# Decoder layer on one core: one-transfer query maxima, a ninth weight slot, weight loads spread over the last batch, and the router's mask in PSUM

## The reference

```python
x = x + mixer(layernorm(x))            # cumulative sums over tokens, low-rank products
x = x + xattn(layernorm(x), ctx_512)   # 16 heads of 32, softmax(Q K^T / sqrt(32)) V, Wo
x = x + ffn(layernorm(x))              # 32 experts

# ffn, per batch:
probs = softmax(x @ gate_w.T + gate_b, axis=tokens)
vals, idx = top 8 tokens of each expert
merged = sum over the 8 of vals * x[idx]              # one vector per batch and expert
h = gelu([merged, 1] @ w1)     # w1: (32, 513, 2048)
o = [h, 1] @ w2                # w2: (32, 2049, 512)
out[idx] += vals * o
```

## Time and profile before

| | us |
|---|---|
| median of 3 runs (2260.3 to 2263.67) | 2262.58 |
| the profiled execution | 2257.76 |
| its span, first to last instruction | 2256.1 |
| PE / DVE / ACT / POOL busy in the span | 1858.3 / 1028.3 / 745.9 / 823.6 |
| DMA moved | 421.34 MB, mean 187 GB/s |

### The profile page before, as it was taken

One profiled execution on the slowest core, in us unless ns is written; L12 is line 12 of the kernel. 1 busy time (PEld: TensorE's weight loads), 2 busy tenths in 40 slices (PEclk: granted clock), 3 DMA queues, 4 the chain that ended last, 5 costly groups with the idle time before them and its releaser, 6 DMA issues. The chain is left out here.

```text
span 2256.1 us, 41492 instructions
## 1 busy us (share of the span) xinstructions
PE 1858.3 (82%) x12594; PEld 1211.7 (54%) x12594; DVE 1028.3 (46%) x2541; ACT 745.9 (33%) x1551; POOL 823.6 (37%) x591
## 2 busy tenths in 40 slices
PE   7889999999999999999999999976756656556544
PEld 5667777677677776777777777753211111111111
DVE  1355766667667666666676666642100000000003
ACT  3144444445445444454454543532100000000000
POOL 0255555545555555465555555543000000000000
PEclk9799999999999999999999999977878787787776
DMA  5324333333243243332432433364899999999996
GB/s 172 88 67 109 78 77 95 82 87 95 74 106 77 76 97 81 89 96 74 103 78 76 99 80 82 80 223 146 367 418 421 421 420 423 422 420 421 422 377 252
DMA packets 143265, 421.34 MB, mean 187 GB/s; under 512 B 33036, under 2 KB 79084, under 8 KB 118652
## 3 DMA queue, kind: packets, MB, share of 16 engines
q1 hardware_dynamic: 135580, 411.70, 53.4%
q10 hardware_dynamic: 6656, 8.15, 1.0%
q0 software_dynamic: 992, 1.02, 0.1%
HBM read 307.37 MB, written 17.14 MB: 144 GB/s over the span
## 5 line engine op out<-in xcount | busy, mean ns | idle before, releaser
L1139 DVE TENSOR_REDUCE maxes<-bank 112x1 f32<-112x376 f32 (+1 forms) x1024 | 511.1, 537 | 129.6 <-PE bank L1345 127.0
L943 ACT ACTIVATE probs<-bank 125x448 f32<-125x448 f32 x768 | 399.5, 546 | 156.9 <-PE bank L1367 150.0
L1367 PE MATMUL bank<-q_st,k_st 98*125 98x224 f32 x1536 | 338.6, 307 | 23.5 <-DMA q_st<-max_lo 21.9
L821 POOL TENSOR_TENSOR psum_keys<-psum_keys,probs 125x896 f32<-125x896 f32 x127 | 266.6, 2099 | 214.9 <-ACT probs L943 209.8
L1345 PE MATMUL bank<-k_st,q_st 96*112 96x376 f32 (+1 forms) x1024 | 319.6, 358 | 21.5 <-DVE maxes L1139 18.9
L1753 PE MATMUL bank<-ring,hid_T 128*32 128x512 f32 x1024 | 175.5, 848 | 194.2 <-DMA ring<-in_L_ffn_w 191.0
L1367 PEld LDWEIGHTS bank<-q_st,k_st 98*125 98x125 f32 x1536 | 258.3, 192 | 82.2 <-issue 48.1
L1671 DVE TENSOR_TENSOR o_fin<-bank,b_row 16x512 f32<-16x512 f32 x32 | 21.7, 679 | 586.0 <-PE bank L1711 586.0
L824 POOL TENSOR_TENSOR psum_keys<-psum_keys,probs 125x896 f32<-125x896 f32 x127 | 266.7, 2100 | 9.9
L1593 POOL DMA_DIRECT2D o_rows<-o_fin x31 | 15.2, 492 | 597.7 <-DVE o_fin L1671 597.7
L1345 PEld LDWEIGHTS bank<-k_st,q_st 96*112 96x112 f32 x1024 | 170.2, 181 | 77.9 <-DVE maxes L1139 50.3
(11 more groups left out here) (168 smaller groups left out, 2762.4 us busy)
## 6 DMA issues: line engine op xcount, KB each, us to landing
ring<-in_L_ffn_w SPq DMA_DIRECT2D x128, 2048.0 KB, 30.4
k_st<-k_hi SPq DMA_DIRECT2D x512, 93.8 KB, 2.1
k_st<-k_lo SPq DMA_DIRECT2D x256, 93.8 KB, 2.2
q_st<-q_hi SPq DMA_DIRECT2D x504, 28.0 KB, 1.8
ctx_nat<-in_ctx SPq DMA_DIRECT2D x16, 750.0 KB
x_in<-in_x SPq DMA_DIRECT2D x16, 448.0 KB, 3.7
out<-x SPq DMA_DIRECT2D x16, 448.0 KB, 3.1
out<-ring ACTq DMA_DIRECT2D x28, 256.0 KB, 3.0
```

Of the source, the lines that this page charges most:

```text
L821: nc.gpsimd.tensor_tensor(psum_keys[:], psum_keys[:], lo, ALU.add).then_inc(pool_chain, 1)
L943: nc.scalar.activation(probs[n % 2][:, j, :], bank[5 + u % 2][0:SK, 0:2 * T], ACT.Exp, scale=SCALE).then_inc(probs_ready, 1)
L1139: nc.vector.tensor_reduce(maxes[:, j, t, c:c + 1], score_bank(n)[0:TT, 0:SC[c + 1] - SC[c]], AX.X, ALU.max).then_inc(s_drained, 1)
L1367: last = nc.tensor.matmul(bank[5 + u % 2][0:SK, kk * T:(kk + 1) * T], k_st[slot][:, j, k * SK:(k + 1) * SK], q_st[slot][:, j, :], start=Tr ...
```

## The change

Four things:

1. *Maxima in one transfer.* `join_maxima` writes each maximum twice ([112, 16]), `turn_max` gives 16 partitions, and `max_rows` makes one tile `max_two` whose first 8 partitions are the high part and whose last 8 are the low part (a column `low_half` of zeros and ones tells them apart). `stack_max` moves both rows with one transfer.
2. *Mask in PSUM.* `beaten` is now the second half of the PSUM bank in which the job `gate` left the logits.
3. *Ninth slot.* `wv_lo`, `ctx_lo`, `xh` and `bias_row` move into a ninth slot of the ring (`EXTRA`). In the last batch SP also loads expert 2's first chunk there, so that 9 chunks are in before the experts start; the turn for experts 2 and 3 is written out, reads that chunk from the extra slot and doesn't refill slot 0. After that the ninth slot is not used.
4. *Order of loads and of the experts' start.* The last batch's loads go out as 0, 1, 2 in group 0, 3, 4 in group 1, 5 and the extra one in group 2, 6 in group 3, each behind the first unit of its group, and 7 after the last unit. `tok` is cleared in the first phase; DVE takes both tokens first; PE turns the biases after the first expert's first matrix.

```diff
+                def extra_weight():
+                    sp.wait_ge(yt_ready, 2 * B)
+                    sp.wait_ge(x_bias_ready, B)
+                    sp.wait_ge(chunk_in[0], 16)
+                    load_chunk(sp, 2, 0, None, 0)
+                def last_batch_weights(kt):
+                    if kt == 0:
+                        sp.wait_ge(x1_ready, 2 * B)
+                        first_weights([0])
...
+                        first_weights([1, 2])
+                    elif kt == 1:
...
+                        first_weights([3, 4])
+                    elif kt == 2:
+                        first_weights([5])
+                        extra_weight()
+                    else:
+                        first_weights([6])
...
+                        if kind == "last":
+                            sp.wait_ge(scores_ready, (LAST * 4 + kt) * 12 + 1)
+                            last_batch_weights(kt)
...
-                        if kind == "last" and kt >= 2:
-                            sp.wait_ge(scores_ready, (LAST * 4 + kt - 1) * 12)
-                            first_weights([2 + kt])
...
-                    for r, part in enumerate((max_hi, max_lo)):
-                        row = 3 * HD + r
-                        act.dma_start(q_st[slot][row:row + 1, :, :].rearrange(
-                            "o j (t n) -> o (j t) n", t=2).bitcast(F32), part[:, :].bitcast(F32)
-                                     ).then_inc(max_stacked[slot], 16)
+                    act.dma_start(q_st[slot][3 * HD:3 * HD + 2, :, :].bitcast(F32),
+                                  max_two[:].bitcast(F32)
+                                  ).then_inc(max_stacked[slot], 16)
...
+                def beaten(kind):
+                    return bank_of("gate", kind)[0:E, T:2 * T]
...
-                    nc.vector.scalar_tensor_tensor(out=weight[0:E, :], in0=beaten[:], scalar=NEG,
+                    nc.vector.scalar_tensor_tensor(out=weight[0:E, :], in0=beaten(kind), scalar=NEG,
...
-                    nc.vector.tensor_reduce(q_max[:], maxes[:].rearrange("p j t c -> p (j t) c"),
+                    twice = maxes[:].rearrange("p j t c -> p (j t) c").unsqueeze(1)
+                    nc.vector.tensor_reduce(q_max[:].rearrange("p (r q) -> p r q", r=2),
+                                            twice.to_broadcast([TT, 2, 8, 2]),
                                             AX.X, ALU.max).then_inc(q_max_ready, 1)
...
-                    nc.vector.tensor_scalar(max_hi[:], bank[4][0:8, 0:TT], -1.0, None, ALU.mult
-                                            ).then_inc(max_hi_ready, 1)
-                    dve.wait_ge(max_hi_ready, g + 1)
-                    nc.vector.scalar_tensor_tensor(out=max_lo[:], in0=bank[4][0:8, 0:TT],
-                                                   scalar=-1.0, in1=max_hi[:].bitcast(F32),
-                                                   op0=ALU.mult, op1=ALU.subtract
-                                                   ).then_inc(max_ready, 1)
+                    nc.vector.tensor_copy(max_hi[:], bank[4][0:16, 0:TT]).then_inc(max_hi_ready, 1)
+                    dve.wait_ge(max_hi_ready, g + 2)
+                    nc.vector.scalar_tensor_tensor(out=max_two[:], in0=max_hi[:].bitcast(F32),
+                                                   scalar=low_half[:, 0:1],
+                                                   in1=bank[4][0:16, 0:TT], op0=ALU.mult,
+                                                   op1=ALU.subtract).then_inc(max_ready, 1)
...
-                with sp.Fori(1, E // 2 - 1) as i:
+                weights(1, 0, False, (1, 2, 3))
+                weights(1, 1, False)
+                with sp.Fori(2, E // 2 - 1) as i:
...
                 take(0, 0, True)
+                take(0, 1, True)
...
+                expert(1, 0, False, EXTRA)
+                expert(1, 1, False)
```

More of the change, by code:

```diff
@@ L109, in build @@
     assert N_MID % 2 == 0
+    assert all(q.index("wt0") - q.index("gate") <= 2 for q in (SEQ["mid"], SEQ["last"], SEQ["tail"]))
     def place(job, kind):
@@ L155, in build, with home_of @@
         SLOTS = 8
+        EXTRA = 4
+        def home_of(slot):
+            return slot if slot < EXTRA else slot + 1
         D1, H1 = KD * P, H
@@ L437, in _, with load_chunk @@
                                                 ).then_inc(s_lo, 1)
-        def load_chunk(sp, e, q, slot):
+        def load_chunk(sp, e, q, slot, told=None):
             n = 2 * H
+            done = chunk_in[slot if told is None else told]
+            slot = home_of(slot) if told is None else EXTRA
             if q < 2:
@@ L444, in load_chunk @@
                 sp.dma_start(ring[:, slot, :], src[:, q * n:(q + 1) * n]
-                             ).then_inc(chunk_in[slot], 16)
+                             ).then_inc(done, 16)
                 return
@@ L492, in build @@
         z_mix = sb(lay, "z_mix", [P, T])
-        beaten = z_mix[0:E, :]
         weight = sb(lay, "weight", [P, T])
@@ L1632, in _ @@
             def _(dve):
-                for c in range(HC):
-                    part = slice(c * 32, (c + 1) * 32)
-                    nc.vector.tensor_copy(adder[part, :], ident[part, part]
-                                          ).then_inc(adder_ready, 1)
-                dve.wait_ge(b1_flipped, 1)
-                nc.vector.tensor_copy(b1_T[:].rearrange("p t c e -> p (t c e)"), bank[4][:]
-                                      ).then_inc(b1_ready, 1)
                 dve.wait_ge(cleared, 1)
@@ L1674, in _ @@
                 take(0, 0, True)
+                take(0, 1, True)
+                for c in range(HC):
+                    part = slice(c * 32, (c + 1) * 32)
+                    nc.vector.tensor_copy(adder[part, :], ident[part, part]
+                                          ).then_inc(adder_ready, 1)
+                dve.wait_ge(b1_flipped, 1)
+                nc.vector.tensor_copy(b1_T[:].rearrange("p t c e -> p (t c e)"), bank[4][:]
+                                      ).then_inc(b1_ready, 1)
                 add_biases(0, 0, True)
-                take(0, 1, True)
                 row_out(0, 0, True)
@@ L1696, in _, with flip_biases @@
             def _(pe):
-                pe.wait_ge(b1_loaded, 16 * HC)
-                for t in range(HT):
-                    last = nc.tensor.transpose(bank[4][:, t * P:(t + 1) * P],
-                                               b1_rows[:].rearrange("e (p t) -> e t p", t=HT)[:, t, :],
-                                               ident[:])
-                last.then_inc(b1_flipped, 1)
-                pe.wait_ge(adder_ready, HC)
+                def flip_biases():
+                    pe.wait_ge(b1_loaded, 16 * HC)
+                    for t in range(HT):
+                        last = nc.tensor.transpose(
+                            bank[4][:, t * P:(t + 1) * P],
+                            b1_rows[:].rearrange("e (p t) -> e t p", t=HT)[:, t, :], ident[:])
+                    last.then_inc(b1_flipped, 1)
                 def sum_parts(i, e2, first):
@@ L1708, in sum_parts @@
                     pe.wait_ge(o_copied, e + 1)
-                    if not first:
+                    if first:
+                        pe.wait_ge(adder_ready, HC)
+                    else:
                         pe.wait_ge(o_out, e)
@@ L1712, in sum_parts, with expert @@
                                      start=True, stop=True).then_inc(o_summed, 1)
-                def expert(i, e2, first):
+                def expert(i, e2, first, extra=None):
                     e = i * 2 + e2
@@ L1723, in expert @@
                             pe.wait_ge(chunk_in[slot], i * 16 + 16)
+                        slot = home_of(slot)
+                        if extra is not None and kd < 2:
+                            slot = extra
                         for c in range(HC):
@@ L1730, in expert @@
                     last.then_inc(h_full, 1)
+                    if first and e2 == 0:
+                        flip_biases()
                     if e2 == 1:
```

71 lines of the change are left out of this document (34 added, 37 removed).

## The result

The changed kernel takes 2225.88 us (median of 4 runs, 2225.29 to 2228.49) against 2262.26 us (2260.3 to 2263.67) for the kernel before: ratio 0.9842, 95% interval 0.9825 to 0.9859. It is 36.4 us faster where 24.7 were forecast, and 2225.9 lies just under the range's lower end of 2227. A second measurement later gave 2228.48 against 2259.05 us, ratio 0.9875 (0.9847 to 0.9903). The profiled executions are 2225.70 us (span 2224.0) and 2257.76 us (span 2256.1): 32.1 us apart.

What follows compares the result with a forecast made beforehand. PE's stalls were taken to bound the mid batches, DMA bytes and the stream's start the experts. Terms 3.1 (maxima), 13.3 (mask), 2.7 (last batch) and 5.6 us (experts) sum to 24.7 off 2262.6: 2238 us, range 2227 to 2251.

Steps and rivals of the forecast that it cites:

- One transfer for the maxima: Mid batches, maxima moved by one transfer instead of two: 0.2 us off in 14 batches, 0.3 once, 3.1 us in all.
- The pin: Third group of a mid batch: ACT's first exponential waits for POOL's sum, so PE's fourth unit gains 0.24 us only.
- outer bound: Third group of a mid batch: the most PE's fourth unit could gain from faster maxima, 0.54 us.
- The +0.4 us for the transfer: Maxima in mid batches: the new two-row transfer itself takes 0.4 us longer, between bounds of 0 and 0.9.
- The mask: Router's product with its mask in PSUM takes 0.36 to 0.40 us: 13.3 us off in the mid batches.
- The last batch: Waits for the maxima shrink by 0.6, 0.7 and 0.4 us, the one on `weight` by 1.0: 2.7 us off.
- The rival that the last batch runs free: Maxima go ahead of chunk 0, 6 us of stall go, clock stays up: some 8 us more, 2230 us; 12%.
- The start of the experts and the ninth chunk: Experts' phase: start 2.8 us sooner, stream one chunk (5.0 us) shorter, less 2.2 us of idle DMA: 5.6 us off.
- hole: Between the first and second refill at the experts' start: DMA engines idle some 2.2 us.
- the sign named beforehand: Expert phase from its barrier to the end 5 to 6 us shorter; if not, the forecast counts as wrong.
- The sum: Whole kernel: 3.1 + 13.3 + 2.7 + 5.6 = 24.7 us off the time before, giving 2238 us.
- the reference: Profiled execution before, 2257.76 us, lies 4.8 us below its runs' median; the same relation was expected after the change.

## Why the forecast was wrong

**One transfer for the maxima: the step that failed.** The forecast had ACT's first exponential held by POOL's sum, so that "even an instant transfer moves PE's fourth unit by 0.24 us only". The pin did not exist. The run with the maxima alone has the exponential start inside POOL's sum, and 0.87 us per mid batch go where I took 0.2: 11.2 us instead of 3.1. The "outer bound" of 0.54 was no bound either: the stall shown was 0.54, the third group came 0.62 us sooner, and 0.24 more lay at the first two products of the first group, where PE showed no idle time before either. The +0.4 us for the transfer was also wrong: it is some 0.04 us longer by the queue's packets, and issue to PE's start is 2.13 us with PE no longer waiting.

**The mask.** Mechanism, line and place right; 379 ns were measured where 360 to 400 stood. The size was short by 2.5 us (15.8 instead of 13.3), for the reason of the idle brackets.

**The last batch.** 4.1 us for 2.7, near enough by sum, but by luck: the forecast took it from the waits, and PE's idle time there grew by 1.0 us. The first wait grew to 8.65 us where I took 0.6 off, the next two were right (4.11 and 1.68). The gain is in PE's busy time, 85.2 us instead of 90.3 at a higher granted clock, which the sum did not hold at all; the twelve other profiled executions have 81 to 87 us there, and why is open. I counted the rows on an engine in an idle queue; under load a row takes a turn of 0.63 us, and two engines need eight of them. The rival that the last batch runs free did not come; holding the loads shows what it was worth, 8.4 us in that batch and 6 to 9 at the end.

**The start of the experts and the ninth chunk.** Refill 2.6 us sooner (2.8 forecast), hole about 2 us (2.2), 6.1 us ahead at expert 4 (5.6): right up to there. It held through the 500 us of full queues (5.4 us with three chunks left). At the end 2.6 us remain, so the sign named beforehand, a phase 5 to 6 us shorter, did not come. I did not look at the end of the stream, where 2 KB rows mix with the chunks; which of them takes the 3 us is open.

**The sum.** Mid batches +9.3, last batch +1.4, experts -3.0: 7.7 us in the stretches, of which 0.4 go in the start-up, and 4.3 us from the reference: I took the profiled execution's 4.8 us under the median to hold for the new kernel too. It lay at its own median. The range allowed 7.7 us for the maxima in its working (14 x 0.55), and then did not reach there.

## What to carry to other kernels

A releaser in a timeline is inferred: before a step is costed as pinned by another, look in the code which buffer it really waits for, and whether the same two meet elsewhere in the trace with one running over the other. Idle time in a bracket was a floor here of what a late input costs, not its ceiling (0.98 us shown, 1.17 gained); comparing the start of the same instruction in two traces gives the cost. Few rows on few engines are free in an idle queue and slow beside a stream of large rows (0.18 and 4.1 us here); two engines or eight made no difference in the sum, the order and the time of the stream did. So put a small urgent transfer ahead of the stream, or the stream later, before changing its shape. And a gain in the right total can come from another place than the forecast's: compare idle and busy time apart.

## What the runs showed of the hardware

- A 448-byte row beside a stream of 16 KB rows waits for one of them each time: 0.63 us a row on an engine, 0.02 us without. Sixteen rows on two engines took 0.18 us idle and 4.1 us under load.
- DVE's copy of the tokens took 1.35 us for two beside POOL's memset of another tile and 0.36 us without it. DVE's product with both inputs in SBUF took 1896 ns beside POOL's sum and 379 ns beside the same sum with one input in PSUM.
- PE's granted clock in 1450 to 1480 us, a mixture of 1.2 and 2.4 GHz, was 0.77 with PE idle for 10.2 of the 30 us and 0.88 with 5.1 us: shorter waits alone did not keep it at 1.0.
- The start up to the third group of the second batch, where most of these kernels have the same work, took from 251.44 to 255.87 us in the profiled executions. A single execution can't show a difference of 1 or 2 us; stretches counted from a common instruction can.
